# A block-sparse attention and product-key expert layer on one core: x kept in SBUF with early statistics, doubled buffers in the token stage, another order on GpSimd, and a rearranged last stage

## Chip, core and metric

The kernel runs on one core of a Trainium2 chip. The engines named here are PE (TensorE), DVE (VectorE), ACT (ScalarE), POOL (GpSimd) and SP (SyncE). The metric is the device time of one execution in microseconds. Shown for the kernel before are the median, lowest and highest of 3 runs, and one execution taken by the hardware profiler.

## What is computed

Eight batches of 512 tokens with 256 channels go through one layer. The attention has 16 heads of 16 channels, each with three branches (blocks compressed to one key, the tokens of the four best blocks, a window of 33 tokens) mixed by gates; beside it stand a gated dense layer and product-key experts.

```python
xn = _layernorm(x)
# attention
q, k, v = split_heads(xn @ Wq), split_heads(xn @ Wk), split_heads(xn @ Wv)
k_c = k.reshape(B, H, 32, 256) @ Wck;  v_c = v.reshape(B, H, 32, 256) @ Wcv
logits_c = where(pos >= blk_end, q @ k_c / 4, -1e9);  out_c = softmax(logits_c) @ v_c
tok = tokens of top_k(logits_c, 4)
out_s = softmax(where(tok <= pos, q @ k[tok] / 4, -1e9)) @ v[tok]
out_l = softmax(where(0 <= pos - s <= 32, q @ k / 4, -1e9)) @ v
gates = softmax(q.mean(heads) @ Wg + bg)
attn = (gates[0] * out_c + gates[1] * out_s + gates[2] * out_l) @ Wo
# experts: 2 x top 8 of 64 keys, top 8 of the 64 sums, in each of 4 heads
w = silu(xn @ down[idx].T) * softmax(scores);  experts = w @ up[idx]
mlp = silu(xn @ Fg + fbg) * (xn @ Fu + fbu) @ Fd + fbd
out = x + attn + mlp + experts
```

## The kernel before

The program has four stages. Each is a block of its own, in which every engine has its own instruction stream and waits for the others by semaphores; between two stages all engines meet at a barrier.

**Setup** (lines 245 to 416). SP loads the projection weights, then the small diagonal blocks `wck` and `wcv`, then the 4.3 MB of weights of the unit stage (`wfg` to `wo`, line 284). POOL builds masks and index patterns with memsets and affine selects (helper at line 292). PE transposes and multiplies weights; DVE splits the biases (393 to 398) and copies PE's results out of PSUM.

**Token stage** (420 to 842), one step for each of the 8 batches, with the work of batch `n` = `t` + 1 done in step `t`. DVE takes statistics of x (`statistics`, 650 to 657), ACT takes the square root (591), DVE normalizes into `xn` (663). PE transposes `xn` (765), DVE copies it to `xT` (671), PE makes queries and keys (785) and values (807) and transposes the values (774). ACT copies queries and keys to `qk` (601) and splits each into three bf16 parts: high (605), middle (611), low (616), with POOL's remainders between (571, 581). In even steps PE compresses the keys of two batches (799, from `kP`, line 606), in odd steps the values (from `vT`, line 627), which DVE and PE then bring into `vcs` (715, 817). SP stores everything to DRAM: `s_xt`, `s_qf`, `s_v`, `s_kc` or `s_vc`, `s_gt`, `s_qs`, `s_ks` (helper at 502). `xn`, `rem`, `parts`, `vn` and `vo` have one buffer each, so `split(n)` on ACT waits for the stores of the previous parts. x comes in two buffers; SP starts the next load when a batch is normalized (529).

**Unit stage** (845 to 1788), 32 units of one batch and four heads. Step `t` finishes unit `t` (`n` = `t` + 1 is prepared in it). PE makes the scores of the compressed keys of `n` (`compressed`, into the bank `lc`); DVE multiplies them by the block mask `block_ok` (1342), POOL adds `block_no` (1062), DVE finds the best eight per row with MAX8 (1352), POOL sets up what is to be struck out (1058 to 1071), DVE strikes (1366). PE's `queries` (1571) give scores of all queries with all keys of `n`, head by head, into two PSUM banks that DVE's `block_max` (1334) reads and releases. For unit `t`, DVE multiplies expert weights `mw` (1430), ACT scales them (1208, `share`), POOL adds the four heads to `cw` (1121, `weights`), takes off the double count (1111) and multiplies by the gate (1127). POOL also makes the pair sums `sumxy` (1097) of `n`. The order on each engine is that of the `step` function of the engine.

**Final stage** (1790 to 1897). For each batch the attention rows `ar` are loaded, transposed on PE (1841), copied by ACT to `aT` (1874), multiplied by `wo` on PE (1852), and added by DVE (1893) to the rows `yr` of the other branches, which ACT loads (1867) and, summed, stores to the output.

## Time and profile before

| | us |
|---|---|
| median of 3 runs (lowest, highest) | 1778.67 (1777.25, 1783.29) |
| profiled execution | 1779.99 |
| its span, first to last instruction | 1778.3 |
| setup, up to SP's first load of x | 29.1 |
| token stage, up to its last store landing | about 237 |
| unit stage, up to SP's last store | about 1722 |
| final stage, to the end | from 1724 |

The page's chain of waits names only the final stage, since it is followed back from the last instruction to the DMA issues on ACT's queue at 1724 us; the stages before are read from windows, waits and timelines.

### The profile page before, as it was taken

The numbers are of one execution on the slowest core, as the hardware profiler recorded it, in microseconds if no ns is written. First come the engines' busy times: TensorE is split into PE (matmuls) and PEld (weight loads), VectorE is DVE, ScalarE is ACT, GpSimd is POOL, SyncE is SP. The second block draws the span as 40 slices with busy tenths as digits, with TensorE's granted clock in tenths as the row PEclk, the third lists the DMA queues.
The fourth block names the chain that finished last, engine by engine and source line by source line (L and its number), as shares of the span: only waits on it lengthen the run. The fifth ranks groups of instructions, "written<-read, shape, count | busy, mean of one in ns | idle before, by whom it ended". The sixth has DMA issues, their size and how long they took to land. (4 is left out here: it accounts for less than half of the span.)

```text
span 1778.3 us, 42038 instructions
## 1 busy us (share of the span) xinstructions
PE 1572.6 (88%) x14000; PEld 1151.6 (65%) x14096; DVE 1171.4 (66%) x4539; ACT 988.7 (56%) x1784; POOL 973.9 (55%) x886
## 2 busy tenths in 40 slices
PE   3888849999999999999999999999999999999877
PEld 2565526666666666666666666666666666666657
DVE  3444357677777777777777777777777777777712
ACT  0666515566566556555555555555566655555541
POOL 4444445556565556565666665666655656556620
PEclk8889969999999999999999999999999999999989
DMA  6445430111111111111111111111111111111026
GB/s 190 144 161 173 168 111 26 30 39 35 31 35 37 37 35 37 34 37 37 37 37 37 37 37 37 37 37 37 37 37 37 37 37 37 37 37 38 8 69 222
DMA packets 151611, 105.09 MB, mean 59 GB/s; under 512 B 63336, under 2 KB 145688, under 8 KB 151576
## 3 DMA queue, kind: packets, MB, share of 16 engines
q1 hardware_dynamic: 143128, 96.27, 18.2%
q10 hardware_dynamic: 8448, 8.39, 1.4%
q8 instruction: 18, 0.29, 0.1%
q14 instruction: 17, 0.14, 0.0%
...
## 5 line engine op out<-in xcount | busy, mean ns | idle before, releaser
L1097 POOL TENSOR_TENSOR sumxy<-xy 128x1024 f32<-128x1024 f32 x128 | 241.0, 1904 | 0.0
L1334 DVE TENSOR_REDUCE bmax<-q_bank 128x32 f32<-128x512 f32 (+3 forms) x512 | 223.9, 486 | 22.2 <-PE q_bank L1571 19.6
L1571 PE MATMUL q_bank<-ko,qo 96*128 96x512 bf16 (+3 forms) x512 | 147.4, 315 | 97.7 <-DVE bmax L1334 97.7
L1187 ACT ACTIVATE pts<-k_bank 128x512 f32<-128x512 f32 (+2 forms) x384 | 181.0, 491 | 83.4 <-PE k_bank L1607 78.9
L1121 POOL TENSOR_TENSOR cw<-cw,mw 128x1024 f32<-128x1024 f32 x64 | 150.3, 2348 | 111.1 <-ACT mw L1208 111.1
L1121 POOL TENSOR_TENSOR cw<-mw 128x1024 f32<-128x1024 f32 x32 | 75.0, 2344 | 205.6 <-ACT mw L1208 205.6
L1430 DVE SCALAR_TENSOR_TENSOR mw<-sumxy,c,ex 128x1024 f32<-128x1024 f32 x128 | 176.3, 1397 | 5.7 <-ACT ex L1202 3.2
L1553 PE MATMUL f_bank<-xt,wfg 128*128 128x128 f32 x1024 | 171.8, 299 | 1.8
L1553 PE MATMUL f_bank<-xt,wfu 128*128 128x128 f32 x1024 | 172.9, 295 | 0.0
L1553 PEld LDWEIGHTS f_bank<-xt,wfu 128*128 128x128 f32 x1024 | 160.0, 209 | 11.9
L1553 PEld LDWEIGHTS f_bank<-xt,wfg 128*128 128x128 f32 x1024 | 153.9, 208 | 12.4
L1247 ACT ACTIVATE qo<-k_bank 32x512 bf16<-32x512 f32 x128 | 75.4, 589 | 136.0 <-PE k_bank L1714 133.8
L1202 ACT ACTIVATE ex<-sumxy,nmax 128x1024 f32<-128x1024 f32 x128 | 142.9, 1141 | 6.2 <-DVE mw L1430 3.1
L1208 ACT ACTIVATE mw<-mw,erec 128x1024 f32<-128x1024 f32 x128 | 145.8, 1139 | 0.0
L1724 PE MATMUL y_bank<-wfd,hT 128*128 128x256 f32 x512 | 138.9, 394 | 1.8
L1352 DVE MAX8 top<-lc 128x8 f32<-128x32 f32 x512 | 50.6, 177 | 129.2 <-issue 129.2
L1607 PE MATMUL k_bank<-qo,ko 128*128 128x384 bf16 (+3 forms) x480 | 130.5, 316 | 0.0
L1738 PE MATMUL y_bank<-wup,cwT 128*128 128x256 f32 x512 | 124.4, 386 | 0.0
L1571 PEld LDWEIGHTS q_bank<-ko,qo 96*128 96x128 bf16 x512 | 52.0, 102 | 110.1 <-DVE bmax L1334 106.8
L1561 PE MATMUL f_bank<-wdn,xt 128*128 128x512 f32 x256 | 121.3, 596 | 0.0
L1194 ACT ACTIVATE ptl<-k_bank 128x512 f32<-128x512 f32 x128 | 76.4, 597 | 79.4 <-remote 50.5
L1357 DVE TENSOR_REDUCE lmax<-q_bank 128x8 f32<-128x512 f32 x64 | 43.5, 691 | 99.8 <-PE q_bank L1593 99.8
...
## 6 DMA issues: line engine op xcount, KB each, us to landing
...
```

The source lines that it names most:

```text
L1097: done("sum_done", g_.tensor_tensor(sumxy[:, h, :, :], xy[:, 0, h, 0:XK, None].broadcast_to([P, XK, KEYS]), xy[:, 1, h, None, :].broadcast ...
L1121: done("cw_sum", g_.tensor_tensor(cw[:, :], mw[:, 0, :] if h == 1 else cw[:, :], mw[:, h, :], ALU.add))
L1187: last = s.activation(pts[:, h, OFFS[j]:OFFS[j] + n], bank[:, 0:n], ACT.Exp)
L1202: done("ex_done", s.activation(ex[:, h % 2, :], sumxy[:, h, :, :].rearrange("p a b -> p (a b)"), ACT.Exp, bias=nmax[:, h:h + 1]))
L1208: done("ms_done", s.activation(mw[:, h, :], mw[:, h, :], ACT.Copy, scale=erec[:, h:h + 1], accum_out=csm[:, h:h + 1]))
L1334: last = v.tensor_reduce(bmax[:, i, h, 0:n], Q.bank(job)[:, o:o + n * BLK].rearrange("p (n j) -> p n j", j=BLK), AX.X, ALU.max)
L1430: done("mw_done", v.scalar_tensor_tensor(mw[:, h, :], sumxy[:, h, :, :].rearrange("p a b -> p (a b)"), c8[:, h, 7:8], ex[:, h % 2, :], ALU ...
L1553: last = mm(dst, w_[:, c, o:o + P], xt[:, t.half, c, :], start=False, stop=(c == 1), skip_group_check=True)
L1571: last = mm(bank[:, o:o + n], qo[0:SP3, t.half, h, P * i:P * i + P], ko[0:SP3, t.half, h, 0:n], start=True, stop=(i > 0))
L1607: last = mm(bank[0:m, o:o + n], ko[:, t.half, h, P * i:P * i + m], qo[:, t.half, h, P * i:T], start=True, stop=True)
L1724: mm(Y.bank("y")[:, 0:C], hT[:, f, :], wfd[:, f, :], start=(f == 0), stop=False)
L1738: last = mm(Y.bank("y")[:, 0:C], cwT[:, e, :], wup[:, e, :], start=False, stop=(e == 7))
```

## The change

- **x**: all eight batches are loaded in the setup into `xin` (batch 0 first of all, 1 to 7 after the projection weights), and DVE takes their statistics there. ACT takes the square roots, one for batch 0 and one for the other seven. Batch 0 is normalized in the setup, the others in the token stage, before the values of the batch ahead.
- **Setup**: ACT issues the small loads and copies PE's results out of PSUM. PE waits for each weight by itself. POOL's masks of which the token stage needs none (`onehot`, `block_ok`, `block_no`, `window_ts`, `tile_of`) are built in the token stage, ahead of POOL's loop. The weights of the unit stage are loaded among the last stores of the token stage.
- **Token stage**: `parts` has two buffers, and the stores of `xt`, `qf`, `parts` and `gt` are counted for each half by itself. SP stores the parts of batch `t` after the tokens of `n`. In odd steps the compression comes before the values of `n`. Both halves of the compressed values are produced before DVE reads the first. DVE's stream is written out, without a loop.
- **Unit stage**: on POOL, the block mask and the selection of `n` stand ahead of all three adds of `weights`. Six of the first loads (`ko` of unit 0) are on ACT's queue. Before batch 7's units SP loads `ar` of batch 0.
- **Final stage**: SP issues all loads, `ar` and `yr` of a batch in turn, and then the stores; PE and DVE wait for both loads of a batch.

The diff, cut to its core:

```diff
+        ar0 = sb("ar0", [P, TT, C])
...
+        xin = sb("xin", [P, B, TT, C])
+        xn = sb("xn", [P, TT, C])
+        stats = sb("stats", [P, B, TT, 6])
+        mv = sb("mv", [P, B, TT, 2])
+        std = sb("std", [P, B, TT])
+        rstd = sb("rstd", [P, B, TT])
+        eps = sb("eps", [P, 1])
+        _, _, sem = make(projecting)
+        xn_ready = Signal(sem("xn_ready"), TT)
+        xv = x.rearrange("b (i p) c -> b p i c", p=P)
+
+        def normalize(b):
+            for i in range(TT):
+                nc.vector.tensor_scalar(xn[:, i, :], xin[:, b, i, :], mv[:, b, i, 0:1], rstd[:, b, i:i + 1],
+                                        ALU.subtract, ALU.mult).then_inc(xn_ready.sem, 1)
...
+                for dst, src, to in (
+                        (xin[:, 0, :, :], xv[0], batch_in[0]),
+                        (wq[:, :, :], Wq.rearrange("(a p) n -> p a n", p=P), wq_in),
+                        (rq[:, :, :], Rq.rearrange("(a p) n -> p a n", p=P), rq_in),
+                        (kn[:, :, :], keys.rearrange("(a h) k p n -> (h k) a (p n)", a=2), kn_in),
+                        (dn[:, :, :], down.rearrange("(a p) n -> p a n", p=P), dn_in),
+                        (wk[:, :, :], Wk.rearrange("(a p) n -> p a n", p=P), proj_in),
+                        (wv[:, :, 0:C], Wv.rearrange("(a p) n -> p a n", p=P), proj_in),
+                        *((xin[:, b, :, :], xv[b], batch_in[b]) for b in range(1, B)),
+                        (bgb[:, :], bg.rearrange("(o n) -> o n", o=1).broadcast_to([P, 3]), proj_in)):
+                    sp.dma_start(dst, src).then_inc(to, 16)
...
+                sp.wait_ge(proj_in, 3 * 16)
...
+                def statistics(b):
+                    dve.wait_ge(batch_in[b], 16)
+                    for i in range(TT):
+                        last = v.bn_stats(stats[:, b, i, :], xin[:, b, i, :])
+                    ch.link(last)
+                    for i in range(TT):
+                        last = v.bn_aggr(mv[:, b, i, :], stats[:, b, i, :])
+                    last.then_inc(var_ready, 1)
+                statistics(0)
+                dve.wait_ge(std_ready, 1)
+                ch.link(v.reciprocal(rstd[:, 0, :], std[:, 0, :]))
+                normalize(0)
+                for b in range(1, B):
+                    statistics(b)
+                dve.wait_ge(std_ready, 2)
+                v.reciprocal(rstd[:, 1:B, :], std[:, 1:B, :])
...
+                def deviation(first, last):
+                    act.wait_ge(cleared, 1)
+                    act.wait_ge(var_ready, last)
+                    nc.scalar.activation(std[:, first:last, :], mv[:, first:last, :, 1], ACT.Sqrt,
+                                         bias=eps[:, 0:1]).then_inc(std_ready, 1)
+
+                def copy(dst, src, **kw):
+                    return nc.scalar.activation(dst, src, ACT.Copy, **kw)
+                deviation(0, 1)
...
+            parts = sb("parts", [P, 2, 2, 3, 2, T], BF16)
...
-                def step(t, n, after):
+                        store("parts", row(dst, n.index).rearrange("r (h p) t -> p r h t", h=2), parts[:, n.half, a, :, :, :], n.half)
+
+                def step(t, n):
                     i = t.index
-                    if after:
-                        sp.wait_ge(xn_ready.sem, xn_ready.at(t))
-                        sp.dma_start(xin[:, t.half, :, :], row(xv, i + 2)).then_inc(x_in[t.half], 16)
                     if n:
                         store_tokens(n)
+                    store_parts(t)
                     if n:
...
+                lots = {4: ((wfg, Fg),), 5: ((wfu, Fu), (wfd, Fd)), 6: ((wup, up), (wo, Wo)), 7: ()}
+                for i in range(B - 4, B):
+                    t = Turn(i // 2, i % 2, tail=(i == B - 1))
+                    step(t, None if t.tail else t.next())
+                    for dst, src in lots[i]:
+                        sp.dma_start(dst[:, :, :], src.rearrange("(a p) n -> p a n", p=P)).then_inc(units_in, 16)
+                sp.dma_start(bdb[:, :], fbd.rearrange("(o n) -> o n", o=1).broadcast_to([P, C])).then_inc(units_in, 16)
...
+                g.memset(onehot[:, :], 1.0)
+                g.memset(block_ok[:, :, :], 1.0)
+                g.memset(block_no[:, :, :], 0.0)
+                g.memset(window_ts[:, :, :], 0.0)
+                ch.link(g.memset(tile_of[:, :, :], 1.0))
...
                 def split(n):
 
-                    act.wait_ge(stored["qf"].sem, stored["qf"].before(n))
-                    act.wait_ge(stored["parts"].sem, stored["parts"].before(n))
+                    stored_before(act, "qf", n)
+                    stored_before(act, "parts", n)
...
                         split(n)
-                    if after:
-                        deviation(after)
                     act.wait_ge(gate_in.sem, gate_in.at(t))
...
                 def step(t, n, after):
                     if n:
                         tokens(n)
+                    gates_in(t)
                     if after:
-                        statistics(after)
-                    gates_in(t)
+                        normalize(after.index)
+                    if t.half == 1:
+                        compressed(t)
                     if n:
                         values(n)
-                    if after:
-                        normalize(after)
-                    compressed(t)
+                    if t.half == 0:
+                        compressed(t)
                     gates_out(t)
                     if t.half == 1:
                         compressed_values(t)
-                steps(dve, step, lead)
+                for i in range(B):
+                    t = Turn(i // 2, i % 2, tail=(i == B - 1))
+                    step(t, t.next() if i + 1 < B else None, t.next(2) if i + 2 < B else None)
 
...
                     if n:
                         queries_keys(n)
+                    if t.half == 1:
+                        compress(t, n)
+                    if n:
                         values(n)
-                    compress(t, n)
-                    if t.half == 1:
+                    if t.half == 0:
+                        compress(t, n)
+                    else:
                         compressed_values(t)
                 steps(pe, step, lead)
...
+                load_near(0, 0, 0)
+                load_parts(0, 0, 0, keys=False)
+                load_late(0, 0, 0)
+                load_near(0, 1, 1)
+                load_parts(0, 1, 1)
+                load_late(0, 1, 1)
...
+                sp.wait_ge(S["st_at"].sem, 16 * (G + 1))
+                sp.dma_start(ar0[:, :, :], s_o[0].rearrange("i p c -> p i c")).then_inc(batch_in[0], 16)
...
                     n = None if t.tail else t.next()
-                    weights(t, (1,))
                     if n:
                         compressed(n)
                         selection(n, now=t)
-                    weights(t, (2, 3))
+                    weights(t, (1, 2, 3))
...
+                k_first = s_ks.rearrange("b r (g h d) t -> b g r d h t", g=G, d=D)[0][0]
+                for n, r in enumerate(K_ROWS):
+                    act.dma_start(ko[D * n:D * n + D, 0, :, :], k_first[r]).then_inc(parts_in[0], 16)
...
+                sp.wait_ge(batch_in[0], 32)
+                sp.dma_start(yr[0][:, :, :], ys[0]).then_inc(batch_in[0], 16)
                 for b in range(1, B):
-                    sp.dma_start(ar[:, b, :, :], s_o[b].rearrange("i p c -> p i c")).then_inc(a_in[b], 16)
+                    sp.dma_start(ar[b][:, :, :], s_o[b].rearrange("i p c -> p i c")).then_inc(batch_in[b], 16)
+                    sp.dma_start(yr[b][:, :, :], ys[b]).then_inc(batch_in[b], 16)
+                sp.wait_ge(armed, 1)
+
+                def step(t, n):
+                    R.wait_read(sp, t, "o1")
+                    sp.dma_start(ov[t.index], yr[t.index][:, :, :]).then_inc(done, 16)
+                steps(step, lambda n: None)
+                sp.wait_ge(done, 16 * B)
...
-                    pe.wait_ge(a_in[n.index], 16)
+                    pe.wait_ge(batch_in[n.index], 48 if n.index else 32)
...
-                ys = s_y.rearrange("(b i) p c -> b p i c", i=TT)
-                for b in range(B):
-                    act.dma_start(yr[:, b, :, :], ys[b]).then_inc(y_in[b], 16)
...
-                    R.wait_read(act, t, "o1")
-                    act.dma_start(ov[t.index], yr[:, t.index, :, :]).then_inc(done, 16)
```

POOL in the loop of the unit stage, at its head: `lc` is the masked score tile, `cw` the sum of expert weights, `mw` the four heads' weights. Before:

```order
L1121 TENSOR_TENSOR cw<-mw 128x1024 [waits ms_done]
L136 ISA
L1062 TENSOR_TENSOR lc<-lc,block_no 128x16x32 [waits q_read0]
L944 ISA
L1058 TENSOR_TENSOR pad<-pad 128x1 [waits top_done]
L1068 COPY strike<-top 128x16x4
L132 ISA
L1071 TENSOR_TENSOR pc<-lc,top 128x512 [waits k_full0]
L944 REGISTER_ALU
L944 ISA [waits ms_done]
L1121 TENSOR_TENSOR cw<-cw,mw 128x1024 [waits cw_sum]
```

POOL at the same place after:

```order
L1098 TENSOR_TENSOR lc<-lc,block_no 128x16x32 [waits q_read0]
L975 ISA
L1094 TENSOR_TENSOR pad<-pad 128x1 [waits top_done]
L1104 COPY strike<-top 128x16x4
L132 ISA
L1107 TENSOR_TENSOR pc<-lc,top 128x512 [waits k_full0]
L975 ISA
L1157 TENSOR_TENSOR cw<-mw 128x1024 [waits ms_done]
L975 REGISTER_ALU
L975 ISA [waits ms_done]
L1157 TENSOR_TENSOR cw<-cw,mw 128x1024 [waits cw_sum]
```

The first add has moved from ahead of the mask to behind the selection; the rest of POOL's step stands as before.

ACT in the loop of the token stage, from the end of the even half's parts to the first copy of the odd half's batch (`gl` are the gates, `std` the deviations). Before:

```order
L590 ISA
L591 ACT_TABLE_LOAD
L591 ACTIVATE std<-mv,eps 128x4 [waits var_ready]
L633 REGISTER_ALU
L634 ACT_TABLE_LOAD
L634 ACTIVATE gl<-gl 128x12 [waits gate_in]
L616 ACTIVATE parts<-rem 128x1024 [waits rem_mid] x2
L627 ACTIVATE vT<-tbank 128x32x16 [waits t_full2]
L627 ACTIVATE vT<-tbank 128x32x16 [waits t_full3]
L595 REGISTER_ALU
L596 REGISTER_ALU [waits st_qf]
L601 ACTIVATE qk<-tbank 128x512 [waits t_full4,st_parts]
```

ACT at the same place after:

```order
L678 ISA
L679 ACTIVATE gl<-gl 128x12 [waits gate_in]
L665 ACTIVATE parts<-rem 128x1024 [waits rem_mid] x2
L674 ACTIVATE vT<-tbank 128x32x16 [waits t_full2]
L674 ACTIVATE vT<-tbank 128x32x16 [waits t_full3]
L498 REGISTER_ALU
L498 REGISTER_ALU [waits st_qf0]
L650 ACTIVATE qk<-tbank 128x512 [waits t_full4,st_parts0]
```

The square root and both table loads are gone, and the wait for the stored parts is one on this half's buffer.

SP at the end of the unit stage and in the final stage. Before:

```order
L1021 DMA s_o<-at 128x4x64 [waits at_done]
L1024 DMA s_y<-yo 128x256 [waits y_read0]
L841 UNCONDITIONAL_BRANCH [waits st_y,st_at]
L1820 UNCONDITIONAL_BRANCH [waits barrier_Pool_Activation_PE_DVE_SP_release]
L1822 DMA ar<-s_o 128x4x256
L1824 DMA ar<-s_o 128x4x256 x7
L1797 UNCONDITIONAL_BRANCH
```

SP in the final stage after (the pair of L1863 and L1864 stands seven times):

```order
L1861 DMA yr<-s_y 128x4x256 [waits batch_in0]
L1863 DMA ar<-s_o 128x4x256
L1864 DMA yr<-s_y 128x4x256
...
L1869 DMA out_dram<-yr 128x4x256 [waits f_free3,armed_f]
L1869 DMA out_dram<-yr 128x4x256 [waits f_free3] x7
L1835 UNCONDITIONAL_BRANCH [waits res_stored]
```

SP has taken over ACT's eight loads and eight stores, with the loads of a batch side by side.

## Rows read from the trace of the kernel before

**Rows 1.** Windows by stage: engine busy (instructions), PE clock, DMA share, GB/s.
```profile
14.00:18.10 4.10, 2.82 (x12) 2.08 (x12) 3.86 (x7) 0.00 (x0) 3.62 (x10) 1.00 0.35 32
36.00:237.00 201.00, 154.50 (x672) 110.01 (x672) 85.06 (x280) 118.88 (x136) 76.67 (x48) 0.87 0.46 156
1724.00:1738.00 14.00, 1.94 (x8) 1.57 (x8) 0.00 (x0) 0.00 (x0) 0.00 (x0) 0.52 0.93 300
```

**Rows 2.** Waits, 300 to 1700 us: who for whom, total us, times, longest.
```profile
PE q_bank L1571 <- DVE bmax L1334: 84.5, 30, 3.3
...
DVE top L1352 <- issue: 123.8, 30, 4.3
```

**Rows 3.** Timeline of a unit: start, us, engine, line, operation, [idle before <-releaser].
```profile
824.26 0.68 DVE L1342 TENSOR_TENSOR lc<-q_bank,block_ok 128x512 f32<-128x512 f32 x1
828.92 0.19 DVE L1352 MAX8 top<-lc 128x8 f32<-128x32 f32 x1 [3.98 <-issue]
...
832.32 0.68 DVE L1318 SCALAR_TENSOR_TENSOR hT<-hT,f_bank 128x512 f32<-128x512 f32 x1
...
836.87 0.69 DVE L1325 TENSOR_TENSOR hT<-hT,f_bank 128x512 f32<-128x512 f32 x1 [0.95 <-PE f_bank L1553]
...
825.30 2.34 POOL L1121 TENSOR_TENSOR cw<-mw 128x1024 f32<-128x1024 f32 x1 [6.83 <-ACT mw L1208]
827.61 1.27 POOL L1062 TENSOR_TENSOR lc<-lc,block_no 128x512 f32<-128x512 f32 x1
...
831.93 2.34 POOL L1121 TENSOR_TENSOR cw<-cw,mw 128x1024 f32<-128x1024 f32 x1
...
833.65 0.39 PE L1571 MATMUL q_bank<-ko,qo 96*128 96x256 bf16 x1 [2.80 <-DVE bmax L1334]
```

**Rows 4.** Windows of one unit and of thirty.
```profile
799.81:844.84 45.03, 42.06 (x412) 30.64 (x412) 33.28 (x133) 26.91 (x52) 26.68 (x24) 0.96 0.13 37
...
297.18:1663.96 1366.78, 1276.40 (x12243) 933.00 (x12330) 997.43 (x3961) 807.10 (x1531) 815.57 (x721) 0.95 0.13 36
```

**Rows 5.** Window behind PE's stand in that unit.
```profile
834.00:836.00 2.00, 2.00 (x13) 1.44 (x13) 1.92 (x19) 0.59 (x1) 0.28 (x1) 0.50 0.00 0
```

**Rows 6.** Waits of ACT, 42 to 237 us.
```profile
ACT qk L601 <- DMA s_ks<-parts: 27.7, 7, 5.5
```

**Rows 7.** Timeline of the token stage, PE and DVE.
```profile
58.19 1.06 PE L774 MATMUL tbank<-ident,vn 128*128 128x128 f32 x8
...
84.95 1.29 DVE L671 COPY xT<-tbank 128x512 f32<-128x512 f32 x2
...
116.12 3.60 PE L785 MATMUL tbank<-xT,wk 128*128 128x512 f32 x8
...
119.55 3.67 PE L807 MATMUL tbank<-wv,xT 128*128 128x259 f32 x16
...
123.46 3.84 PE L799 MATMUL tbank<-kP,wck 128*128 128x128 f32 x32 [0.24 <-ACT kP L606]
...
202.90 1.48 DVE L671 COPY xT<-tbank 128x512 f32<-128x512 f32 x2 [0.50 <-PE tbank L765]
```

**Rows 8.** Timeline of the setup and the first batch.
```profile
11.44 4.82 POOL L292 TENSOR_SCALAR_AFFINE_SELECT tile_of<-tile_of 32x512 bf16<-32x512 bf16 x6
...
37.59 1.41 DVE L652 BATCH_NORM_STATS2 stats<-xin 128x6 f32<-128x256 f32 x4 [9.26 <-DMA xin<-in_L_attn_x_dram]
...
44.95 3.75 PE L785 MATMUL tbank<-xT,wq 128*128 128x512 f32 x4 [0.83 <-DVE xT L671]
...
52.36 2.12 POOL L571 TENSOR_TENSOR rem<-qk,parts 128x1024 f32<-128x1024 f32 x1 [21.65 <-ACT parts L605]
```

**Rows 9.** Timeline of the final stage's start.
```profile
1724.04 13.97 ACTq L1867 DMA_DIRECT2D yr<-s_y  x8
...
1729.28 1.94 PE L1841 MATMUL fbank<-ident,ar 128*128 128x128 f32 x8 [10.05 <-DMA ar<-s_o]
...
1738.85 1.51 PE L1841 MATMUL fbank<-ident,ar 128*128 128x128 f32 x6 [7.63 <-ACT aT L1874]
```

279 lines of the change are left out of this document (117 added, 162 removed).

## The prediction, made before the changed kernel was run

> **What bounds the kernel now.** I read the stages first, by windows of engine time. The unit stage, 32 units of attention and experts, is 77% of the span: from the GpSimd instruction that closes unit 0's weights to the one that closes unit 30's lie 1366.78 us [rows 4], 30 units of 45.56 us. PE is busy for 93% of it at a clock of 0.95. The token stage (36 to 237 us) has PE busy 154.5 of 201 us at clock 0.87, and in 1724 to 1738 PE works 1.94 of 14 us while DMA runs at 300 GB/s [rows 1].
>
> Next the waits of 300 to 1700 us. PE has one wait worth the name: 84.5 us in 30 waits for DVE's block maxima, 2.8 us a unit. DVE has one that is larger still: 123.8 us in 30 before its MAX8 over the masked scores [rows 2], put down to "issue", which only says that no data producer ended just then. The timeline of one unit tells whose it is [rows 3]. DVE writes the product with the block mask at 824.26 to 824.94. GpSimd has just begun an add of expert weights at 825.30, and gets to the mask's second half (`lc`) only at 827.61; that ends at 828.88, and DVE's MAX8 starts at 828.92. DVE then has struck-out blocks, a gate and the maxima behind it, and PE stands until 833.65 for a PSUM bank those maxima release. After the stand PE's clock is 0.50 in 834 to 836 us [rows 5]: the level of 1.2 GHz, where a unit otherwise runs at 2.4.
>
> **Unit stage: GpSimd's order.** The change lets `lc` (1.27 us) and the selection go ahead of the first add, which joins the other two. `lc` then starts when DVE's product is there, 825.0 instead of 827.61, and MAX8 2.6 us earlier, at 826.35. The price is the add's 2.34 us: it now starts after the selection's last operation, about 829.4, and the second follows at 831.7 instead of 831.93, the third when its share is ready as before. So no consumer of `cw` waits longer; its cover is the idle time of GpSimd before the third add (it waits there for ScalarE's share); without it 2.34 us would reach DVE's expert sum.
>
> Does PE become the bound, or does DVE stay it? PE: it is busy 42.06 us of a unit of 45.03 at a mean clock of 0.96 [rows 4]. At full clock that shrinks by at most 4% of 45.03, 1.8 us, so PE alone needs about 40.3 to 40.7 us. DVE and GpSimd hand work to each other in a ring: DVE's expert sum, GpSimd's candidates and pair sums, DVE's shifts and experts, GpSimd's `lc`, MAX8, and round to the expert sum. It is closed but for two idle spots: 3.98 us before MAX8, of which 1.4 stays (`lc` itself), and 0.95 us before DVE's second hidden product at 836.87, which waits for a PE matmul behind PE's stand [rows 3]. The stand gone, that matmul comes over 3 us earlier and the 0.95 goes. Ring: 45.03 - 2.57 - 0.95 = 41.5 us. It is longer than PE's 40.7, so DVE stays the bound by under a microsecond, and PE meets two or three stands of 0.3 to 0.5 us a unit. I take those as too short to lower the clock. All 31 units with a successor have this step: 31 x (45.56 - 41.5) = **-125.6 us**. Bounds: 40.7 us a unit if the ring is looser than I think (-151); 43 if PE's clock still falls once a unit (-79).
>
> **Start: statistics in the setup.** Before, DVE's first statistics wait until 37.59 us for x, which is queued behind the 4 MB of weights of the units, and the first query matmul starts at 44.95 [rows 8]. After, batch 0 is loaded first and normalized in the setup. The setup becomes longer, though: at 300 GB/s [rows 1] the 3 MB ahead of batch 1's x are through at 12 us and that x at about 13.8; seven statistics on DVE at 1.41 us plus about half a microsecond of aggregation take 13.3 us, to 27; deviation and reciprocal make 27.8, and then the bias operations, DVE's 3.86 us in 14 to 18.1 us [rows 1], end near 31.8. Barrier and GpSimd's semaphore increments put the first transposes at 34.1 and the query matmul at 37: **-8.0 us**. Bounds: -11 if SyncE's 16 small loads end it (about 28.5), -5 if x arrives late. ScalarE takes over the copies out of PSUM; batch 0 needs its 14 small loads, and is done by 20, under DVE's cover.
>
> GpSimd's masks move out of the setup into the token stage: 17 selects like the six that take 4.82 us, plus memsets, 14.9 us in all [rows 8]. Its first remainder is wanted 7.4 us after the query matmul (52.36 against 44.95), 44.4 in the new time; it is free at 49. That is 4.6 us late, of which ScalarE's and PE's waits swallow some: I charge 3 us in the first batch.
>
> **Token stage.** Two waits belong to what is removed. ScalarE waits 27.7 us in 7 for the store of `s_ks`, whose single buffer the next batch overwrites [rows 6], and DVE waits for each batch's x, as in the start [rows 8]. Two buffers of `parts` take the first away, x in SBUF the second, and with the square roots gone ScalarE reloads its tables once in two batches, not five times. What is late next is PE: queries and keys 3.6 each, values 3.67, compression 3.84, two lots of transposes of 1.06 each [rows 7], and I add 0.6 for the compressed values: 17.4 us a batch. On top I count 2.1 us in two batches where ScalarE's reload and the previous low parts (behind GpSimd's copy of `vo`) hold up `kP`, 1 us where DVE's gate work stands ahead of the copy of `xT`, and some low clock: 19.6 us a batch. Before, batch 2 to batch 7 took from 84.95 to 202.90 [rows 7], 118 us, 23.6 each. Five steps: -20.0. Up to batch 2 I put the waits that go at 4.2 us (one on the store, one table load, one on x) and the masks' charge at 3, -1.2; at the end both halves of the compressed values in one bank pass and an earlier remainder give -1.5. **-22.7 us**. Bounds: 17.8 a batch (-32), and 22 (-10) if the weights' 4.3 MB, now queued among the last stores, hold back buffers.
>
> Loads of unit 0's keys on ScalarE's queue: 0, since PE is then still at the scores of `wsim`. The copy of the first attention rows in batch 7 is one DMA of half a microsecond on SyncE between units whose loads are a unit ahead: 0.
>
> **Final stage.** ScalarE issues eight loads in 13.97 us and copies nothing before; PE's second transposes wait for it until 1738.85. The first began at 1729.28, when 1.05 MB were in [rows 9]. After, `ar` of batch 0 is in SBUF, ScalarE copies at once, and PE's second transposes need three loads of 0.52 MB from one queue: 1729.28 plus 1.5 us for the third, 1730.8. From there the pace is PE's as before, with 12 MB to move by 1774, 250 GB/s. **-8.0 us**; bounds -4 (stores, queued behind 15 loads on SyncE, come last) and -9.
>
> **Sum.** 1778.3 - 125.6 - 8.0 - 22.7 - 8.0 = 1614.0 span. The profiled run was 1779.99, 1.7 above its span, and 1.3 above the median of 1778.67. So 1614.0 + 1.7 - 1.3 = **1614.4 us**.
>
> **Rivals.**
> *1. The clock keeps falling.* PE has no slack left, and two or three short stands a unit might lower the clock as the 2.8 us did. For it: nothing in the unit stage shows PE with short stands alone. Against: where it falls in a unit now, a stand of 2.80 us is what went before [rows 3, 5]. Price 1.5 us a unit, 43.0: 1661 us. The Trainium skill, "TensorE: Matmul & The Clock Gate", in "A second HAM failure mode", tells of a kernel whose PE idles briefly between groups while cycling PSUM banks and whose clock swings between the levels; by that this rival would be the rule. No row here decides it.
> *2. The port.* GpSimd's three adds now run back to back beside DVE's strikes, gates and maxima. If each held DVE up for all its length, 3 x 2.34 = 7.0 us, the ring would be 48.5 us, 2.9 above today: 31 x 2.9 = +91 less 38.7 of the other stages, 1831 us. It decides for **slower** from 5.2 us of the 7.0 on. Against: the add at 831.93 already runs beside DVE's gate at 832.32, which takes 0.68, the same as the 0.69 of the product at 836.87 with GpSimd idle [rows 3]. The Trainium skill, "SBUF — State Buffer", in "Who interferes with whom", has an exclusive lock between the two for operations with two SBUF inputs or two-port modes only; what stands there in this stretch reads PSUM.
> *3. The wait only moves.* MAX8 comes earlier but PE's bank is held by something else (GpSimd's expert chain, ScalarE's shares in head 1): no more than 1 us a unit. 1614 + 31 x 3.06 = 1709 us. The ring's other waits speak against it, all tied to DVE's own shift.
> *4. The unit gain comes, the token stage gives nothing*, its stores and GpSimd being the bound: 1614 + 23 = 1637 us.
>
> **Chances.** Forecast 0.58 (own range 1594 to 1632), rival 1 0.20, rival 4 0.10, rival 3 0.07, rival 2 0.02, something faster than 1594 0.03. The range, 1594 to 1663, takes in rivals 1 and 4. A change of 0.3% is about what a measurement can tell from none; faster 0.97, same 0.01, slower 0.02.
>
> **What would show it.** In the trace of after: `lc` within 0.2 us of DVE's product, DVE's wait before MAX8 about 1.4 us, PE's longest wait in a unit under 0.7 and its clock near 1.0, units of 41.5; a clock below 0.97 is rival 1, longer DVE operations beside the adds rival 2. First query matmul at 37, batches of 19.6 with no ScalarE wait on a store, PE's second transposes 7 us after the last barrier. Wrong above all if the ring has a member that I read as tied to DVE and is tied to PE's or a DMA's time.

## The result and the profile after

| | before | after |
|---|---|---|
| median, us (lowest, highest) | 1777.96 (1776.81, 1783.29) of 4 runs on the same chip | 1611.76 (1610.88, 1612.61) of 4 runs |
| ratio, 95% interval | | 0.906 (0.904 to 0.908) |
| profiled execution and its span | 1779.99, 1778.3 | 1612.61, 1610.8 |

The time fell by 166 us, a little more than the 164 us predicted (1614.4), and lies in the range. That the total came within 2 us is luck: it hides a unit stage that gave 9.7 us more than forecast and a token stage that gave 7.0 less. Four landmarks split the spans: the first query matmul of the token stage, the first matmul of the unit stage, PE's last matmul of the unit stage, and the end. Those of before, in the timeline of PE (start, us, engine, line, operation, and in brackets its idle time before and what ended it), the first beside [rows 8]:

```profile
241.82 0.55 PE L1664 MATMUL q_bank<-kc,qf 64*128 64x128 f32 x1 [7.49 <-DMA xt<-s_xt]
...
1718.63 0.60 PE L1657 MATMUL k_bank<-ident,oT 128*128 128x128 f32 x4
```

And after, in the same view (PE's second transposes of the final stage, 1570.91, answer to the last of [rows 9]):

```profile
35.70 1.19 PE L810 MATMUL tbank<-xT,wq 128*128 128x512 f32 x1 [0.83 <-DVE xT L695]
...
216.87 2.04 PE L1702 MATMUL q_bank<-kc,qf 64*128 64x128 f32 x8 [10.77 <-DMA xt<-s_xt]
...
1558.38 0.60 PE L1695 MATMUL k_bank<-ident,oT 128*128 128x128 f32 x4
1564.13 1.97 PE L1888 MATMUL fbank<-ident,ar 128*128 128x128 f32 x8 [5.15 <-POOLq L1877]
1570.91 1.97 PE L1888 MATMUL fbank<-ident,ar 128*128 128x128 f32 x8 [4.81 <-DMA yr<-s_y]
```

| stretch | before | after | change | predicted |
|---|---|---|---|---|
| start, to the first query matmul | 44.95 | 35.70 | -9.25 | -8.0 |
| token stage, to the unit stage's first matmul | 196.87 | 181.17 | -15.7 | -22.7 |
| unit stage, to its last matmul | 1476.81 | 1341.51 | -135.3 | -125.6 |
| the rest, to the end | 59.67 | 52.42 | -7.25 | -8.0 |
| span | 1778.3 | 1610.8 | -167.5 | -164.3 |

**Unit stage.** The windows that answer to [rows 4] (engine busy times, PE's clock, DMA share, GB/s), from unit 0's last weight to unit 30's, and of one unit:

```profile
268.00:1506.45 1238.45, 1222.19 (x12242) 894.03 (x12330) 989.70 (x3961) 802.43 (x1531) 818.30 (x720) 1.00 0.14 41
845.89:887.02 41.13, 40.71 (x411) 29.80 (x412) 32.89 (x133) 26.76 (x52) 27.70 (x25) 1.00 0.14 40
```

1238.45 us are 30 units of 41.28 us (41.13 and 41.43 in turn), where the sum had 41.5. PE's clock is 1.00 over the whole stretch. The waits of 300 to 1700 us (total, times, longest), against [rows 2]:

```profile
DVE lmax L1395 <- PE q_bank L1631: 96.4, 30, 3.2
...
DVE top L1390 <- issue: 40.4, 29, 1.4
...
PE q_bank L1609 <- DVE bmax L1372: 11.3, 45, 0.6
```

DVE's wait before MAX8 is 1.4 us, as forecast. PE's wait for the block maxima is 11.3 us in 45, none over 0.6 us, where it was 84.5 in 30. The unit's timeline, against [rows 3]:

```profile
870.07 0.68 DVE L1380 TENSOR_TENSOR lc<-q_bank,block_ok 128x512 f32<-128x512 f32 x1
872.14 0.19 DVE L1390 MAX8 top<-lc 128x8 f32<-128x32 f32 x1 [1.39 <-issue]
...
875.53 0.68 DVE L1356 SCALAR_TENSOR_TENSOR hT<-hT,f_bank 128x512 f32<-128x512 f32 x1
...
879.26 0.69 DVE L1363 TENSOR_TENSOR hT<-hT,f_bank 128x512 f32<-128x512 f32 x1
...
870.83 1.27 POOL L1098 TENSOR_TENSOR lc<-lc,block_no 128x512 f32<-128x512 f32 x1 [5.35 <-DVE lc L1380]
...
875.16 2.37 POOL L1157 TENSOR_TENSOR cw<-mw 128x1024 f32<-128x1024 f32 x1
...
881.63 0.28 PE L1609 MATMUL q_bank<-ko,qo 96*128 96x256 bf16 x1 [0.25 <-DVE bmax L1372]
```

GpSimd's mask half starts 0.08 us behind DVE's product, the adds of expert weights run behind the selection, DVE's gate and product beside them take 0.68 and 0.69 us as before, and the 0.95 us ahead of the second product are gone. PE's stand (its idle time before an operation) is 0.25 us.

**Token stage.** DVE's copies of `xT` mark the batches; the first of these rows is batch 2, the last batch 7, against [rows 7]. The others show PE and DVE at the start of batches 3 and 7, and GpSimd beside them:

```profile
73.07 1.29 DVE L695 COPY xT<-tbank 128x512 f32<-128x512 f32 x2
...
172.23 2.04 DVE L752 TENSOR_TENSOR gl<-gl,any_ok 128x4 f32<-128x4 f32 x1
...
174.86 1.27 DVE L695 COPY xT<-tbank 128x512 f32<-128x512 f32 x2
...
172.13 4.21 POOL L633 TENSOR_TENSOR rem<-rem,parts 128x1024 f32<-128x1024 f32 x2
...
94.69 6.43 PE L810 MATMUL tbank<-xT,wq 128*128 128x512 f32 x8 [3.42 <-DVE xT L695]
```

and, of the waits of 30 to 212 us:

```profile
PE tbank L810 <- DVE xT L695: 16.8, 7, 3.4
```

Five steps took 101.8 us, 20.4 each instead of 23.6, but not 19.6. PE waits 16.8 us in 7 for `xT`, 2.4 us a batch where I had counted 1. After such a stand the query matmuls of batch 3 take 6.43 us for 3.67; after the same stand of 3.42 us those of batch 5 take 3.67.

Runs 2 to 6 and 12 below leave the token stage as it is, so that there are seven traces of it. The stage takes 174.9 to 181.2 us in them, 178.7 in the mean: the -15.7 of the table is the smallest gain of the seven, the largest is -22.0, the mean -18.2.

### The profile page after: what moved, and what is told of

Read it like the earlier page. It is cut to its first block and busy times, and to the rows that moved or that the text cites. A ratio compares the mean times of both kernels' runs of the same rounds, so it can differ in the third digit from the quotient of the medians.

```text
span 1610.8 us, 41888 instructions
## 1 busy us (share of the span) xinstructions
PE 1510.3 (94%) x14000; PEld 1103.4 (68%) x14096; DVE 1152.5 (72%) x4511; ACT 974.8 (61%) x1780; POOL 976.3 (61%) x886
## 5 line engine op out<-in xcount | busy, mean ns | idle before, releaser
L1372 DVE TENSOR_REDUCE bmax<-q_bank 128x32 f32<-128x512 f32 (+3 forms) x512 | 217.4, 482 | 3.3 <-PE q_bank L1609 1.1
L1609 PE MATMUL q_bank<-ko,qo 96*128 96x512 bf16 (+3 forms) x512 | 142.9, 306 | 21.9 <-DVE bmax L1372 21.9
L1591 PE MATMUL f_bank<-xt,wfg 128*128 128x128 f32 x1024 | 158.6, 282 | 1.8
L1591 PE MATMUL f_bank<-xt,wfu 128*128 128x128 f32 x1024 | 158.7, 277 | 0.0
L1098 POOL TENSOR_TENSOR lc<-lc,block_no 128x512 f32<-128x512 f32 x32 | 40.7, 1273 | 186.5 <-DVE lc L1380 186.5
L1591 PEld LDWEIGHTS f_bank<-xt,wfu 128*128 128x128 f32 x1024 | 144.5, 191 | 10.0
L1591 PEld LDWEIGHTS f_bank<-xt,wfg 128*128 128x128 f32 x1024 | 139.3, 191 | 10.3
L1645 PE MATMUL k_bank<-qo,ko 128*128 128x384 bf16 (+3 forms) x480 | 120.2, 293 | 0.0
L1256 ACT ACTIVATE sw<-f_bank 128x512 f32<-128x512 f32 x64 | 38.0, 593 | 120.2 <-PE f_bank L1599 119.6
L1762 PEld LDWEIGHTS y_bank<-wfd,hT 128*128 128x128 f32 x512 | 89.5, 190 | 22.2 <-DVE hT L1363 9.6
```

The source lines that it names most:

```text
L1372: last = v.tensor_reduce(bmax[:, i, h, 0:n], Q.bank(job)[:, o:o + n * BLK].rearrange("p (n j) -> p n j", j=BLK), AX.X, ALU.max)
L1591: last = mm(dst, w_[:, c, o:o + P], xt[:, t.half, c, :], start=False, stop=(c == 1), skip_group_check=True)
L1609: last = mm(bank[:, o:o + n], qo[0:SP3, t.half, h, P * i:P * i + P], ko[0:SP3, t.half, h, 0:n], start=True, stop=(i > 0))
L1762: mm(Y.bank("y")[:, 0:C], hT[:, f, :], wfd[:, f, :], start=(f == 0), stop=False)
```

## The experiments

All are timed beside runs of the kernel before on the same chip, whose medians lie between 1779.6 and 1779.8 us. The length of a unit is taken from GpSimd's first and last subtraction of the last expert weight (`clast`), 29 or 30 units apart; line numbers in rows are those of each kernel.

### 1. The order alone

```
 (before)
-                    weights(t, (1,))
                     if n:
                         compressed(n)
                         selection(n, now=t)
-                    weights(t, (2, 3))
+                    weights(t, (1, 2, 3))
```

> The kernel before with one edit: GpSimd's mask half and selection go ahead of its first add of expert weights. In the changed kernel the unit stage became 135 us shorter (query scores of unit 0 to the last matmul of the stage: 1476.8 us before, 1341.5 after). Theory A, that the order alone does this: units of 41.3 us, PE's clock 1.00 in them, 1778 - 135 = 1643 us. Theory B, that some of it comes from SBUF addresses, earlier loads or the shorter stages around: a smaller gain, units above 41.8 us, 1658 us or more.

1650.38 us (1649.85 to 1650.95), ratio 0.9275 (0.926 to 0.929): 129 us faster than before, with units of 41.33 us. Theory A holds: between its landmarks (242.69 and 1588.33) the unit stage is 131.2 us shorter than before, of the 135.3. Of the other 4.1 us, thirty units make 1.0 and the last unit 3.7, less 0.6 in the first. In the last unit PE stands 2.79 us here, and its clock is 0.50 in 1560 to 1564; before, it stood 3.03 us there, and the clock was 0.60 and 0.55 in 1690 to 1694. In the kernel after it stands 1.31 us and the clock stays at 1.00. The two stands, of run 1 and of after:

```profile
1557.34 0.39 PE L1547 MATMUL f_bank<-tile_of,bias 96*128 96x512 bf16 x1 [2.79 <-DVE sw L1440]
1529.62 0.39 PE L1586 MATMUL f_bank<-tile_of,bias 96*128 96x512 bf16 x1 [1.31 <-DVE sw L1479]
```

What shortened that stand stays open.

### 2. Less work on PE

```
-                    for f in (2 * part, 2 * part + 1):
+                    for f in (2 * part, 2 * part + 1) if part < 3 else ():
                         mm(Y.bank("y")[:, 0:C], hT[:, f, :], wfd[:, f, :], ...)
```

> The changed kernel without the last quarter of the dense layer's down product (its last two 128-row slices; the output lacks them): the four matmul instructions of 1.02 us that stand ahead of the selected values in each unit. Nothing else moves. Two theories of what paces a unit of 41.28 us. A, the prediction's: the ring of VectorE and GpSimd (41.5) is longer than PE's work; then PE gets 1.0 us more of stands, the unit keeps 41.1 to 41.3, and the time is 1606 to 1612. B, read in the trace after: PE is busy for 98.7% of the stage at full clock, so PE paces it; then the unit falls by nearly 1.0 us, to 40.3, and the time by 32 us to 1580. In between: both within half a microsecond of each other, 40.8 and 1596.

1611.65 us (1610.39 to 1615.99): no change, units of 41.28 us. PE's busy time fell, the time did not (window, as above; the first row is of after):

```profile
300.00:1500.00 1200.00, 1184.07 (x11855) 866.45 (x11940) 959.36 (x3850) 778.10 (x1485) 792.97 (x698) 1.00 0.14 41
```

```profile
300.00:1500.00 1200.00, 1159.08 (x11736) 845.36 (x11821) 988.79 (x3840) 776.05 (x1485) 795.88 (x698) 1.00 0.15 41
```

Theory A holds. A PE that is busy 98.7% of the time did not pace the unit: 0.86 us less work a unit (25.0 us in 29 units) turned into idle time. The Trainium skill, "Perfetto Trace Analysis", in "Identifying the Most-Contended Engine", says to optimize the engine of highest occupancy first, but to judge TensorE by its use of peak and by the busy share of its weight loads, not of its matmuls. In the first row the weight loads are busy 866.45 of 1200 us (72%) and DVE 959.36 (80%), so by that measure DVE stands first, and the runs agree with it as far as DVE is on the ring, the round of hand-overs between DVE and GpSimd that must be gone through once a unit. Where the ring closes is seen on DVE and GpSimd behind the window maxima, in the kernel after:

```profile
856.76 1.65 DVE L1422 CAST shift_l<-lmax 128x16 bf16<-128x16 f32 x1
858.44 0.68 DVE L1423 TENSOR_TENSOR shift_l<-lmax,shift_l 128x16 bf16<-128x16 f32 x1
858.99 0.76 DVE L1426 TENSOR_TENSOR bsel<-bmax,unsel 128x512 f32<-128x512 f32 x1
...
860.51 0.18 DVE L1429 CAST smax_hi<-smax 128x16 bf16<-128x16 f32 x1
...
854.59 3.75 POOL L1133 TENSOR_TENSOR sumxy<-xy 128x1024 f32<-128x1024 f32 x2
858.31 0.72 POOL L1167 TENSOR_TENSOR xb<-xb,bdb 128x256 f32<-128x256 f32 x1
```

and with less work on PE:

```profile
854.77 0.66 DVE L1422 CAST shift_l<-lmax 128x16 bf16<-128x16 f32 x1
855.46 1.85 DVE L1423 TENSOR_TENSOR shift_l<-lmax,shift_l 128x16 bf16<-128x16 f32 x1
857.19 1.27 DVE L1426 TENSOR_TENSOR bsel<-bmax,unsel 128x512 f32<-128x512 f32 x1
...
853.47 3.76 POOL L1133 TENSOR_TENSOR sumxy<-xy 128x1024 f32<-128x1024 f32 x2
857.19 0.73 POOL L1167 TENSOR_TENSOR xb<-xb,bdb 128x256 f32<-128x256 f32 x1
```

In the first, the CAST of 16 values takes 1.65 us; another CAST of 16 values, at 860.51, takes 0.18. It ends at 858.41, as GpSimd's two pair sums do (854.59 + 3.75 = 858.34). In the second, the maxima come earlier, the CAST slips in between two pair sums (0.66 us), and the next operation, with two SBUF inputs, stands instead, 1.85 us, until 857.3, as GpSimd's pair sums end; the one behind it takes 1.27 us beside the add of `xb`. What PE gave was lost again at once: the sum with the block maxima ends 1.4 us behind GpSimd's pair sums in the one (859.75, 858.34) and 1.2 us in the other (858.46, 857.23). So DVE's wait for PE's window scores (3.2 us in the first, 2.4 in the second) is not on the ring, and these rows speak for one that runs through GpSimd's pair sums; runs 6 and 12 bear on it.

### 3. The mask's half later by one add

```
                     Q.wait_read(pool, t, "lc")
+                    g_.tensor_tensor(spare, <block_no>, <block_no>, ALU.add)
                     done("lc_done", g_.tensor_tensor(lc ...))
```

> The changed kernel with one more GpSimd add over the same 512 elements (about 1.27 us, result unused) in front of the mask's second half, so that MAX8 comes 1.27 us later in each unit: about half of the 2.6 us that the change took away. If the ring paces the unit, all of it is seen: +1.27 x 32 = 41 us, 1652. If PE paces it and the ring has slack, less: 1620 to 1640, with PE's wait for the block maxima longer by what is missing. If a stand of 1 us or more lowers PE's clock (the prediction's first rival), the clock of the unit stage goes from 1.00 to about 0.97 and the unit to more than 42.8 us, 1660 us or more.

1643.29 us (1642.30 to 1644.28), units of 42.26 us. The added operation took 1.04 us (its output is bf16), and the unit grew by 0.99: all of it is seen. The clock did not fall, though PE now stands up to 1.2 us:

```profile
PE q_bank L1612 <- DVE bmax L1375: 38.3, 58, 1.2
```

```profile
300.00:1480.00 1180.00, 1139.03 (x11403) 832.37 (x11488) 920.51 (x3675) 745.44 (x1422) 787.07 (x697) 1.00 0.14 40
```

### 4. More adds beside the strikes

```
                         done("cw_sum", ...)
+                        if h < 3:
+                            g_.tensor_tensor(spare[:, h - 1], some, some, ALU.add)
```

> The changed kernel with two more GpSimd adds (480 elements each, about 1.2 us, result unused), one behind the first and one behind the second add of expert weights, where VectorE strikes blocks and takes block maxima. GpSimd has 4.5 us of idle time behind its third add, so its own path has room for 2.4 us. Forecast: no change, 1612 plus or minus 2 us. The prediction's second rival (each add holds VectorE up for its length): +2.4 us a unit, 1612 + 75 = 1687 us, and VectorE's operations in that stretch longer.

1610.77 us (1610.70 to 1613.29), units of 41.26 us: no change. The two adds took 0.99 us each and came out of GpSimd's idle time (3.0 instead of 4.5 us before `clast`); DVE's strikes (180 and 179 ns) and block maxima kept their length. Rival 2 is refuted for this stretch: what DVE does there reads PSUM or strikes.

### 5. The small operations moved to GpSimd

```
 (DVE)   -  cn.link(v.tensor_copy(shift_l[:, :, :, 0], lm))
         -  done("shift_done", v.tensor_tensor(shift_l[:, :, :, 1], lm, shift_l[:, :, :, 0], ALU.subtract))
 (GpSimd, behind branches(t))
         +  done("shift_hi", g_.tensor_tensor(shift_l[:, :, :, 0], lm, <zeros>, ALU.add))
         +  done("shift_done", g_.tensor_tensor(shift_l[:, :, :, 1], lm, shift_l[:, :, :, 0], ALU.subtract))
```

> The changed kernel, with the two small operations that make shift_l from the window maxima (16 values a partition, 1.65 and 0.68 us on VectorE in the changed kernel) moved to GpSimd's idle time at the end of its step. Theory L: VectorE's copies and its operations with two SBUF inputs stand while GpSimd runs an add of two SBUF inputs, and this stretch is on the ring that paces the unit. Then VectorE's sum with the block maxima starts when GpSimd's last pair sum ends, 0.7 us earlier than now, and the ring is 40.6 us; PE's 40.7 us of busy time stands below it, so the unit falls to about 40.8 and the time by 31 x 0.45 = 14 us, to 1598. Theory R: the operations are just slow and stand off the ring: within 2 us of 1612.

1610.32 us (1607.07 to 1613.10), units of 41.27 us: nothing in the unit. The forecast from theory L was wrong, yet the rows show the standing operations all the same, at other places:

```profile
853.14 2.27 DVE L1430 TENSOR_TENSOR bsel<-bmax,unsel 128x512 f32<-128x512 f32 x1
...
856.38 1.01 DVE L1435 TENSOR_TENSOR shift_s<-smax,smax_hi 128x16 bf16<-128x16 f32 x1
...
854.82 1.18 POOL L1175 TENSOR_TENSOR xb<-xb,bdb 128x256 f32<-128x256 f32 x1
...
856.25 1.05 POOL L1116 TENSOR_TENSOR pc<-pc,cfac 128x512 f32<-128x512 f32 x1
```

The sum with the block maxima (2.27 us for 0.76) ends 0.6 us behind the pair sums as forecast, but then GpSimd's multiplication by `cfac` holds up the subtraction that makes `shift_s`, 1.01 us for 0.23. Taking away the operations that were held did not help. That the GpSimd work which holds them is the ring fits this, but this run does not show it by itself, since it also gave GpSimd two operations more.

### 6. Candidate sums early

```
 (candidates, behind the mask of xy)
-                    done("cand_done", ...)
 (step; pairs waits for t8_done and makes the candidate sums)
                     weights(t, (1, 2, 3))
+                    if n:
+                        pairs(n)
                     last_expert(t)
```

> The changed kernel, with GpSimd's candidate sums (0.62 us) made in its idle 4.5 us before the sum of the last expert weight instead of behind the mask of xy. VectorE no longer waits 2.25 us for them, and GpSimd's pair sums end 0.62 us earlier. If the ring runs through GpSimd's pair sums, as read from the second run of this study (PE's work shortened by 0.9 us a unit and the unit unchanged), the ring falls by 0.62 to 40.66 us, and PE's 40.7 holds it: 40.8, 1612 - 15 = 1597. If VectorE's wait for the candidates were what closes the ring, up to 2.25 us would go and PE would hold it at the same 40.8. If PE paced the unit: no change.

1602.16 us (1600.00 to 1603.66), 9.6 us less than the kernel after; units of 41.04. That is a gain, but of 0.24 us a unit, 7.4 us in 31, not 0.62 a unit. The rest is not the edit's: the token stage, which it does not touch, is 3.6 us shorter in this trace than in that of after. DVE's wait of 2.3 us for the candidates went as well, and by the forecast either could have closed the ring; this run alone does not tell the two apart.

### 7. The copy of xT ahead of the gates' end

```
                     if n:
                         tokens(n)
+                    if t.index:
+                        gates_out(before[0])
+                    before[0] = t
                     gates_in(t)
 ...
-                    gates_out(t)
+                    if t.tail:
+                        gates_out(t)
```

> The changed kernel, with the end of the gates' work of a batch (four small operations on VectorE) put behind the copy of the next batch's xT in the token stage instead of ahead of it. PE waits 16.8 us in 7 for that copy in the changed kernel, 2.4 a batch, where the prediction had counted 1. If the gates ahead of it are the cause (small operations of 1 to 2 us beside GpSimd's adds), PE's wait falls to about 0.7 a batch and batches take 18.7 instead of 20.4 us: -12 us, 1600. If the stage is then held by ScalarE or by stores, less: 1605 to 1612.

1602.66 us (1602.03 to 1603.20), 9.1 us less than after. PE's wait for `xT` is 0.8 us in all; batches take 19.1 us. What holds them is now ScalarE: in four of eight batches PE waits for `kP`. Behind the waits of 2.93 and 2.95 us the compression takes 6.66 and 5.46 us; behind those of 3.14 and 1.61 it keeps its length (3.84 and 3.81).

```profile
PE tbank L829 <- ACT kP L655: 10.6, 4, 3.1
```

```profile
103.83 6.66 PE L829 MATMUL tbank<-kP,wck 128*128 128x128 f32 x32 [2.93 <-ACT kP L655]
```

### 8. The unit stage's weights loaded in the setup

```
+                for dst, src in ((wfg, Fg), (wfu, Fu), (wfd, Fd), (wup, up), (wo, Wo)):
+                    sp.dma_start(...)     # and bdb, behind the 16 small diagonal blocks
                 sp.wait_ge(proj_in, 3 * 16)
 ... (token stage)
-                lots = {4: ((wfg, Fg),), ...}     # and the loads from it, and bdb
```

> The changed kernel, with the 4.3 MB of weights of the unit stage loaded by SyncE at the end of the setup, behind x, instead of among the last stores of the token stage. In the changed kernel the last store of s_ks took 12 us to land, against 5.9 before, and the unit stage's first matmul came 10.8 us after the token stage's last instead of 7.5. If the weights ahead in the queue are the cause, 3.3 us come back: 1608. If the early loads hold back the token stage's first stores or x: 1612 or more.

1617.44 us (1616.09 to 1619.31), 5.7 us slower than after. `wfg`, `wfu` and `wfd` went out in half a microsecond each, the next two issues took 2.9 and 3.3 us behind them, SyncE was through at 37.0, and the barrier waited for it:

```profile
30.00 2.90 SPq L289 DMA_DIRECT2D wup<-in_L_ffn_up_embed_dram  x1
32.94 3.31 SPq L289 DMA_DIRECT2D wo<-in_L_attn_Wo_dram  x1
...
39.56 1.97 PE L789 MATMUL tbank<-ident,xn 128*128 128x128 f32 x8 [19.27 <-POOLq L589]
```

The transposes start at 39.56 instead of 32.90, 6.7 us later. From `xT` of batch 7 to the unit stage's first matmul it is 40.9 us. In the two traces of the unchanged token stage in which batch 7's query matmuls run as slowly as here (6.63 us in after and 6.66 in run 4, for 6.58) it is 42.0 and 41.7: the weights among the last stores cost about 1 us, not 3.3.

### 9. One buffer for parts

```
-            parts = sb("parts", [P, 2, 2, 3, 2, T], BF16)
+            parts = sb("parts", [P, 1, 2, 3, 2, T], BF16)
 ...
-                    stored_before(act, "parts", n)
+                    stored_last(act, "parts", n)      # the batch before, not the one before that
```

> The changed kernel with one buffer for parts again, so that ScalarE's copies of a batch wait until the parts of the batch before are stored; x in SBUF, the square roots in the setup and the rest stay as changed. The prediction put the token stage's gain of 20 us in five steps down to two waits (ScalarE's on the store, 4 us a batch before; VectorE's on x) and three table loads. If the store's wait is on the path here too, 3 to 4 us come back in each of 7 batches: 1612 + 24 = 1636. If the path was freed by the other two and ScalarE has room, less than 5 us: 1612 to 1617.

1635.47 us (1633.67 to 1636.71), 23.7 us slower than after, as forecast. ScalarE waits longer than ever, against [rows 6]:

```profile
ACT qk L654 <- DMA s_ks<-parts: 52.3, 7, 13.9
```

The wait is 52.3 us here and was 27.7 in the kernel before, and the token stage is longer than before (203.0 us for 196.9). So the 24 us are what the second buffer is worth in the new order, in which the parts are stored behind the next batch's tokens; they are not what the wait cost before.

### 10. The masks late

```
 (GpSimd, token stage)  the block of memsets and selects for onehot, block_ok, block_no,
 window_ts and tile_of moved from ahead of the loop over the batches to behind it
```

> The changed kernel with GpSimd's masks for the unit stage (13.3 us, 33.1 to 46.4 in the changed kernel) built behind its last remainder of the token stage, where it is idle from 196 to 211 us, instead of ahead of its first. The prediction charged them 3 us of path in the first batch. If so, 1609; if ScalarE's and PE's waits in the first batch swallow it, 1612; if the masks outlast the stage's last stores there, later than 1612.

1607.91 us (1603.90 to 1611.94), 3.9 us less than after at the median, but the four runs spread over 8 us, and the intervals of the ratios overlap (0.9005 to 0.9054 here). The masks now take 189.4 to 202.6 us, and GpSimd starts on the unit stage at 206.1. `xT` of batch 7 comes 3.6 us earlier (171.28). This is not the masks' doing in the main: in run 12, which has them where they were, it comes at the same time (171.29). 2.8 of the 3.6 us come between batches 3 and 4, where after the stand of 3.42 us the clock fell in the kernel after (6.43 us, above) and in runs 10 and 12, after stands of 3.43 and 3.41 us, it did not:

```profile
93.88 3.67 PE L810 MATMUL tbank<-xT,wq 128*128 128x512 f32 x8 [3.43 <-DVE xT L695]
```

```profile
93.91 3.67 PE L810 MATMUL tbank<-xT,wq 128*128 128x512 f32 x8 [3.41 <-DVE xT L695]
...
171.29 1.27 DVE L695 COPY xT<-tbank 128x512 f32<-128x512 f32 x2
```

What the masks cost is seen up to batch 2: its `xT` comes 36.7 us behind the first query matmul here, and 36.8 to 37.4 in the seven traces with the masks first, so 0.1 to 0.7 us.

### 11. The findings together

```
   the edits of 6, 7 and 10; wfg and wfu loaded behind batch 4, wfd, wup, wo and bdb behind 5;
   and on GpSimd in the token stage:
         rem = qk - parts (high)          x2
+        rem = rem - parts (middle)       x2
         wait vn_ready; vo = vn
-        rem = rem - parts (middle)       x2
```

> A version built on the findings: the changed kernel with candidate sums early (9.6 us in its own run), the gates' end behind the copy of xT (9.1 us), the masks late, the unit stage's weights one batch earlier in the token stage, and GpSimd's second remainders ahead of its copy of vo, which waits for VectorE's values (ScalarE waits 35.6 us in 16 for these remainders, and PE then waits 2.9 us for kP in every second batch and runs the compression behind it in 6.7 us at half clock instead of 3.8). If the last frees PE: 4 x 4 = 16 us. Sum: 1612 - 10 - 9 - 3 - 16 - 1 = 1573. If ScalarE stays the limit of the token stage: about 1588.

1583.30 us (1582.05 to 1583.49), ratio 0.889 (0.8875 to 0.8904): 28.5 us less than after, better than both kernels. Batches take 17.1 us (`xT` of batch 2 at 71.21, of batch 7 at 156.87), and from batch 3 on PE hardly stands before the compression of the keys (it still stands 3.15 us in the first pair of batches):

```profile
89.83 3.67 PE L816 MATMUL tbank<-xT,wq 128*128 128x512 f32 x8 [0.41 <-issue]
...
100.67 3.84 PE L830 MATMUL tbank<-kP,wck 128*128 128x128 f32 x32 [0.23 <-ACT kP L656]
```

The units are 41.05 us. The forecast of 1573 missed by 10 us; its other case, ScalarE still the limit, was 1588. The likely reason, not tried by itself, is that the gain of 7 and what I gave the new order of remainders were in part the same stands and clock falls, counted twice; and the 3 us from run 10 were not the masks'.

### 12. Candidate sums early and less work on PE

```
   the edits of 6 and 2 together
```

> The version with early candidate sums (units of 41.04 us, 1602.2) without the last quarter of the dense layer's down product (the output lacks it), as in the second run. There the unit did not move when PE's work fell by 0.9 us. With VectorE's wait for the candidates gone, VectorE waits for PE's score banks instead (1.8 us a unit in three waits). If PE has thereby come on the path that paces the unit, the unit falls to the ring's 40.66 us, 1602 - 12 = 1590. If the unit is still GpSimd's and VectorE's alone, it stays at 41.0, 1601 to 1603.

1594.55 us (1590.71 to 1599.90), units of 40.80 us. In run 2 the same cut of PE's work gave nothing; here it gives 0.24 us a unit, and the sum of both edits comes to 40.80, near the 40.66 of a ring that has lost only the 0.62 us from GpSimd's pair sums. DVE's wait for the candidates (2.25 us) is gone here as in run 6; had that wait closed the ring, the unit could have fallen to about PE's own 39.6 us (an estimate: PE is busy 1146.6 of 1180 us here). So the pair sums are the reading that fits, and with the candidates early PE shares the pace. The runs of this kernel spread by 9 us; the length of the unit is the firmer number.

## Why the prediction was right, and where it was off

**Unit stage, right in mechanism and nearly in size.** GpSimd's order alone makes the stage 131 us shorter, of 135 (run 1). The ring was read at 41.5 and measured at 41.28 us: the 2.57 us of MAX8 came as worked out (`lc` within 0.08 us, a wait of 1.39), and the 0.95 us went. The remaining 0.22 us a unit is the sum's small error, 7 us in 31 units; the 32nd unit, in which no successor is prepared, also became 2.7 us shorter (54.67 to 51.93 from unit 30's last weight to PE's last matmul), which I had not counted: PE's clock fell in it before and in run 1, and does not after.

**Which engine paces it, right against the appearance.** "DVE stays the bound by under a microsecond" held: run 2 took 0.86 us from PE and nothing came, run 3 gave the ring 1.04 us and 0.99 came. But the ring had a member that I did not name: by the rows of run 2, DVE's operations that stand behind GpSimd's pair sums. Run 6, which shortens GpSimd's work on it by 0.62 us, gains 0.24, and run 12 shows that PE takes over from there.

**Rival 1, the clock.** It did not happen: 1.00 over 1238 us, with two or three stands of up to 0.6 us a unit, and still 1.00 in run 3 with stands of up to 1.2 us. The Trainium skill, "TensorE: Matmul & The Clock Gate", in "A second HAM failure mode", tells of a kernel whose PE idles briefly between groups and whose clock swings; the unit stage here does not show that, the clock stayed at the level of 2.4 GHz. A chance of 0.20 was rather high: in the token stage of before, batch 6's query matmuls take their full-clock 3.67 us behind a stand of 1.19 us (179.59). That was one stand, not two or three a unit.

**Rival 2, the port.** Refuted where I had placed it (run 4). The Trainium skill, "SBUF — State Buffer", in "Who interferes with whom", excepts operations with at most one SBUF input outside the two-port modes, and those that read PSUM kept their length. "What stands there reads PSUM" was not all of it, though: the strikes read SBUF, and kept theirs too (180 and 179 ns). The turning point of this rival was 5.3 us of the 7.0, not 5.2 (164.3 us in 31 units). I used that section only to dismiss a rival. Applied to every DVE operation with two SBUF inputs or a copy beside GpSimd's adds, it would have led to the CAST of 1.65 us on the ring, and to the token stage's gates.

**Start, -9.25 for -8.0.** Statistics are paced at 1.70 us a batch, where I had 1.9 (`stats` 1.37 and aggregation 0.3 at the margin), which brings the deviation to 27.2 and offsets that x of batch 1 lands at 15.1, not 13.8. The bias operations take 2.7 us, not 3.86. Two timeline rows:

```profile
15.07 1.41 DVE L387 BATCH_NORM_STATS2 stats<-xin 128x6 f32<-128x256 f32 x4 [2.81 <-DMA xin<-in_L_attn_x_dram]
...
29.87 0.68 DVE L406 TENSOR_TENSOR bias<-b 32x512 bf16<-32x512 f32 x1
```

**Token stage, -15.7 for -22.7: the step that was off.** The waits that it named went, and the store's wait is on the path (run 9). Four terms of the sum were mis-sized.

First "1 us where DVE's gate work stands ahead of the copy of `xT`": it is 2.4 us, 16.4 to 16.8 us in 7 in all seven traces, because the gates' last multiplications, 4 and 12 values a partition and 0.17 us by themselves, take 1 to 2 us beside GpSimd's remainders (172.23 above). Run 7 gives back 9 us by order alone.

Second the "some low clock". The difference between two steps with and without a fall shows it: from batch 3 to 4 it is 21.06 us in the trace of after and 18.28 in run 12, from 6 to 7 it is 21.94 and 20.24, and the rest goes the same way (from 5 to 6 it is run 12 that is longer, 19.98 for 18.29). Without falls the five steps would be 97.3 us, 19.5 each. So the forecast of 19.6 was near the batch without falls only because two errors cancel: the wait for `xT` is longer than I had it, and the 2.1 us in two batches for `kP` did not come (0.8 us in all in the trace of after). On top the clock took 4.5 us in the five steps of after, and 1.7 in those of run 12.

Third the masks, charged with 3 us: 0.1 to 0.7 (run 10). The waits that go up to batch 2 are worth about 3.3 us (40.0 us from the first query matmul before, 36.7 in run 10) for the 4.2 that I gave them, and the gain was 2.6 us for 1.2.

Fourth the stage's end: I had -1.5 us, and the stretch from `xT` of batch 7 to the unit stage's first matmul became 3.1 us longer (38.92 to 42.01). Nearly all of it is again the clock: batch 7's query matmuls take 6.63 us behind their stand; in runs 2, 3 and 12, where they take 3.67 behind the same stand, the stretch is 39.7, 39.2 and 39.1 us. The weights among the last stores cost about 1 us (run 8). The six loads on ScalarE's queue, which I had put at 0, were not tried by themselves.

So -2.6, -16.2 and +3.1 make the -15.7 of this trace. The clock falls behind the stands for `xT` come to 4.5 us in the five steps and 3.0 at the end, about what is missing; another execution need not have them, and run 12's stage, with 1.7 of them, came to -22.0. The forecast named some low clock and gave it no size of its own. What decides whether the clock falls behind such a stand stays open.

**Final stage, -7.25 for -8.0.** PE's second transposes start 7.1 us behind SyncE's first issue after the barrier (1563.77), as forecast (7); up to them 7.7 us are gained. Behind them 0.4 us are lost again, since the first product with `wo` takes 4.68 us for 4.12.
